# Attention and a mixture of experts on one core: the weighed V of a block issued one block later, behind the scores

## The reference

```python
x = x + _layernorm(attn(_layernorm(x), Wq, Wk, Wv, Wo))
x = x + _layernorm(ffn(_layernorm(x), router_w, Wg, Wu, Wd, ...))

def attn(x, Wq, Wk, Wv, Wo):
    q, k, v = proj(Wq), proj(Wk), proj(Wv)        # (B, H, S, 32)
    q, k = rope(q), rope(k)
    scores = where(causal, q @ k.T / sqrt(32), -big)
    probs = softmax(scores)
    return (probs @ v) @ Wo.T
```

## Time and profile before

| | before |
|---|---|
| median of 3 runs | 1199.74 us (1198.04 to 1199.86) |
| the profiled execution's own time | 1199.09 us |
| its span | 1197.2 us |
| mean granted TensorE clock | 0.968 |
| PE busy | 1085.3 us (91%) |
| DVE busy | 692.3 us (58%) |
| POOL busy | 621.0 us (52%) |
| ACT busy | 473.2 us (40%) |
| first `turn` and last `weighted` of the attention | 36.92 and 430.4 us |

### The profile page before, as it was taken

One profiled execution on the slowest core, in us unless ns is written; L12 is line 12 of the kernel. 1 busy time (PEld: TensorE's weight loads), 2 busy tenths in 40 slices (PEclk: granted clock), 3 DMA queues, 4 the chain that ended last, 5 costly groups with the idle time before them and its releaser, 6 DMA issues.

```text
span 1197.2 us, 24385 instructions
## 1 busy us (share of the span) xinstructions
PE 1085.3 (91%) x6309; PEld 728.9 (61%) x6310; DVE 692.3 (58%) x2354; ACT 473.2 (40%) x1366; POOL 621.0 (52%) x629
## 2 busy tenths in 40 slices
PE   5799899989999989979869999999999999999964
PEld 3455566555566545555537777777777776767721
DVE  3766566556666668857855454444444444444447
ACT  1566567656666642242202222222222222222213
POOL 4333333333333312200127888888888777778824
PEclk9899999999999999979969999999999999999987
DMA  9600000000000051100157999999999989997796
GB/s 350 241 2 1 4 1 2 2 4 2 1 2 1 2 227 55 62 16 12 60 163 173 223 218 248 244 226 235 258 231 255 242 213 269 259 227 160 113 318 251
DMA packets 65713, 166.81 MB, mean 139 GB/s; under 512 B 15314, under 2 KB 16594, under 8 KB 65504
## 3 DMA queue, kind: packets, MB, share of 16 engines
q0 software_dynamic: 38496, 83.95, 31.8%
q1 hardware_dynamic: 27136, 81.88, 19.4%
HBM read 119.85 MB, written 62.65 MB: 152 GB/s over the span
## 4 chain that ended last, share of the span: by engine, by line
PE 68%; DMA 16%; DVE 9%; issue 3%; ACT 2%; POOL 1%; DVEq 0%; POOLq 0%; ACTq 0%
PE ps L906 14%; PE ps L658 14%; DMA sum_rows<-x_t,idx 9%; PE ps L917 7%; PE ps L717 6%; DMA x_t<-x_rows,idx 5%; PE ps L773 4%; PE ps L687 4%; PE ps L890 4%; PE ps L737 4%; PE ps L672 2%; PE ps L809 2%; PE ps L789 1%; PE ps L825 1%; DVE high L1196 1%
## 5 line engine op out<-in xcount | busy, mean ns | idle before, releaser
L906 PE MATMUL ps<-big,work 128*128 x1264 | 300.5, 381 | 0.0
L430 POOL DMA_INDIRECT sum_rows<-x_t,idx x157 | 249.9, 1591 | 56.4 <-issue 37.4
L906 PEld LDWEIGHTS ps<-big,work 128*128 128x128 f32 x1264 | 229.0, 191 | 24.9
L424 POOL DMA_INDIRECT x_t<-x_rows,idx x159 | 165.9, 1043 | 69.9 <-issue 28.3
L658 PE MATMUL ps<-big 128*128 128x384 f32 x512 | 179.1, 493 | 1.5 <-ACT big L501 1.1
L369 POOL TENSOR_TENSOR work<-qkv_all,rope_sb 128x256 f32<-128x256 f32 x64 | 46.6, 728 | 249.4 <-ACT qkv_all L506 249.3
L612 ACT ACTIVATE work<-ps 128x512 f32<-128x512 f32 x159 | 94.9, 597 | 202.7 <-PE ps L890 200.4
L917 PE MATMUL ps<-big,work 128*128 x314 | 160.7, 593 | 0.3 <-issue 0.3
L890 PEld LDWEIGHTS ps<-ident_sb,x_t 128*128 128x128 f32 x636 | 78.1, 142 | 108.6 <-issue 68.3
L998 DVE CUSTOM_DVE_ANT_0 ps<-ps,mask_sb 128x128 f32<-128x128 f32 (+3 forms) x256 | 120.8, 513 | 24.0 <-PE ps L687 23.4
L523 ACT ACTIVATE work<-ps,neg_max 128x128 f32<-128x128 f32 (+3 forms) x256 | 132.4, 528 | 4.3 <-DVE neg_max L998 3.2
(11 more groups left out here) (176 smaller groups left out, 1455.9 us busy)
## 6 DMA issues: line engine op xcount, KB each, us to landing
big<-experts SPq DMA_DIRECT2D x65, 768.0 KB, 7.3
sum_rows<-x_t POOLq DMA_DIRECT2D x4, 2048.0 KB, 10.6
big<-sum_rows SPq DMA_DIRECT2D x8, 768.0 KB, 10.9
x_sb<-x SPq DMA_DIRECT2D x4, 1024.0 KB, 15.5
x_rows<-work SPq DMA_DIRECT2D x16, 256.0 KB, 2.0
sum_rows<-attn_t POOLq DMA_DIRECT2D x2, 2048.0 KB
out<-x_sb SPq DMA_DIRECT2D x16, 256.0 KB, 5.9
x_t<-sum_rows SPq DMA_DIRECT2D x4, 768.0 KB, 13.5
```

Of the source, the lines that this page charges most:

```text
L424: pool.indirect_dma_start(rows[:, q, :], None, x2_rows, bass.IndirectOffsetOnAxis(ap=idx[:, q, 0:1], axis=0), bounds_check=last_row, oob_i ...
L430: pool.indirect_dma_start(all_sums, bass.IndirectOffsetOnAxis(ap=idx[:, q, 1:2], axis=0), y_sb[:, q, :], None, bounds_check=last_sum, oob_ ...
L906: mm = pe.matmul(ps[:, 2 + p, 0:GATEUP], rows_t[:, p, c, :], w_ring[:, slot, c * GATEUP:(c + 1) * GATEUP], start=(c == 0), stop=(c == DC - 1))
```

## The change

`weigh` of block k-1 is issued in iteration k directly behind `score` of block k+1, in place of `weigh` of block k at the iteration's end; the last block of a batch is weighed at the end of its batch. `weigh` has a new wait, for `s_qkt` up to the copy of block k+2, since it now writes bank 6 behind `qkt`. `qkt` waits no longer for `weighted` of block k-1, but for `evac_rden` of block k-1 and `weighted` of block k-2. `turn_rden` keeps its wait for `weighted` of block k-1. On DVE `weighted` of block k-1 stands between the first and the second `masked` of block k+1. No operation is added or dropped.

```diff
--- before.py
+++ after.py
@@ -659,14 +659,18 @@
                                    start=(c == 0), stop=(c == DC - 1))
                 mm.then_inc(s_qkv_ps, 1)
 
-            def qkt(n, t, k):
+            def qkt(n, t, k, late=False, after=None):
 
                 pe.wait_ge(s_rope, n + 1)
+                if late:
+                    pe.wait_ge(s_rden_t, k)
+                    if after is not None:
+                        pe.wait_ge(s_attn, after)
                 if isinstance(n, int) and n < LEAD_QKT:
                     pe.wait_ge(s_qkv, TB - 1)
                 if not (isinstance(n, int) and n == 0):
                     pe.wait_ge(s_qkt, n)
-                if k is not None and not (isinstance(k, int) and k == 0):
+                if k is not None and not late and not (isinstance(k, int) and k == 0):
                     pe.wait_ge(s_attn, k)
                 for c in range(2):
                     mm = pe.transpose(turn_bank[:, bass.ts(c, P)], roped[:, t % 2, bass.ts(c, P)], ident_sb[:, :])
@@ -725,12 +729,13 @@
                     pe.wait_ge(s_attn, k)
                 pe.transpose(rden_bank, rden[:, :, :].rearrange("p h d -> p (h d)"), ident_sb[:, :]).then_inc(s_rden_ps, 1)
 
-            def weigh(k, i):
+            def weigh(k, i, qkts):
 
                 g, qt = divmod(i, TB)
                 pe.wait_ge(s_pt, (k + 1) * ON_ACT)
                 pe.wait_ge(s_pt_dve, k + 1)
                 pe.wait_ge(s_rden_t, k + 1)
+                pe.wait_ge(s_qkt, qkts)
                 for c in range(qt + 1):
                     for h in range(HG):
                         v0 = 2 * P + DH * h
@@ -743,21 +748,25 @@
 
                 for i in range(BLOCKS):
                     k = b * BLOCKS + i
+                    qkts = b * BLOCKS + min(i + LEAD_QKT + 1, BLOCKS) if last else b * BLOCKS + (i + LEAD_QKT + 1)
                     turn(k, i, 0)
                     turn(k, i, 1)
                     if i + LEAD_QKT < BLOCKS or not last:
-                        qkt(b * BLOCKS + (i + LEAD_QKT), (i + LEAD_QKT) % TB, k)
+                        qkt(b * BLOCKS + (i + LEAD_QKT), (i + LEAD_QKT) % TB, k, late=(i >= 1),
+                            after=b * BLOCKS + (i - 1) if i >= 2 else None)
                     if i + 1 < BLOCKS or not last:
                         score(b * BLOCKS + (i + 1), (i + 1) % BLOCKS)
+                    if i >= 1:
+                        weigh(b * BLOCKS + (i - 1), i - 1, qkts)
                     if i >= BLOCKS - TB and not last:
                         xt((b + 1) * TB, i % TB, qkv_bank)
                     turn(k, i, 2)
                     turn(k, i, 3)
-                    turn_rden(k, b * BLOCKS + min(i + LEAD_QKT + 1, BLOCKS) if last else b * BLOCKS + (i + LEAD_QKT + 1))
+                    turn_rden(k, qkts)
                     if i < BLOCKS - TB or not last:
                         proj(b * BLOCKS + (i + LEAD_PROJ), (i // TB + 1) % G, i % TB, qkv_bank,
                              after_xt=(b + 1) * TB if i >= BLOCKS - TB else None)
-                    weigh(k, i)
+                weigh(b * BLOCKS + (BLOCKS - 1), BLOCKS - 1, qkts)
 
             every_batch(pe, batch)
 
@@ -1033,12 +1042,16 @@
                         take_qkt(b * BLOCKS + j, j // TB % G, j % TB)
                     if more:
                         masked(k1, q1, 0)
+                    if i >= 1:
+                        weighted(b, b * BLOCKS + (i - 1), i - 1)
+                    if more:
                         masked(k1, q1, 1)
                     evac_pt(k, i)
                     if more:
                         masked(k1, q1, 2)
                         masked(k1, q1, 3)
-                    weighted(b, k, i)
+                    if i == BLOCKS - 1:
+                        weighted(b, k, i)
                     if more:
                         invert(k1)
                     if i in NORM_X_AT and not last:
```

## The result

Slower by a third of a percent: 1202.97 us against 1198.04 (medians of 7 runs each), ratio 1.0034 with a 95% interval of 1.0021 to 1.0048. That is 4.1 us by the ratio and 4.9 by the medians. A second set (12 runs against 28) gives 1.0035 (1.0019 to 1.0052); one more run of the kernel before, at 1984.34 us with a granted clock of 0.70, is left out there.

A forecast was written before the change was run, and what follows sets the result against it. The prediction took PE as the chain, packed to about 97% in the attention. Looped batches +1.0, last batch +0.9 and tail +0.9 gave +2.8 us: 1202.5 against 1199.74 us, +0.23%, range 1196.5 to 1207.5.

The forecast's parts named there:

- the slower case: Whole kernel a little slower, as summed: 0.5 to 5 us, chance 0.50; slower in all 0.48.
- The prize: PE's stalls before `qkt`, 0.42 us in q0 and 0.20 in q1, go: some 0.62 us in 23.6 of a group.
- The order of shapes: On PE `proj` is followed by `turn` instead of `weigh`, 2.58 us instead of 2.67: -0.1 a block.
- nothing saved: Rival: the order of shapes on PE saves nothing, +0.1 in 45 blocks, +4.5 us, 1207; chance 0.13.
- the rule of the Trainium skill: Weight loads overlap matmuls in flight only in different row groups, so `turn` behind `proj` on PE would save nothing.
- The stall in front of `weigh`: On PE `weigh` waits for DVE's copy of Q and K behind `invert`: 0.38 us in q3, 0.45 more behind `norm_x`.
- The stall in front of `turn_rden`: On PE `turn_rden` waits for `weighted` of block k-1: 0.42 us in q0, 0.35 in q1, 0.05 in q2, none in q3.
- Late starts: In block 8 of looped batches `weighted` starts 0.34 us later, half taken as lost (-0.17); rival "no difference", chance 0.22.
- The sum: Attention terms together: looped batches +0.33 each, +1.0 for three, last batch +0.9, tail +0.9: +2.8 us.
- tail: Last three blocks, without projection: `weigh` lies behind `score`, in front of the next link of the exps' chain: +0.9 us.
- the first rival: Faster: the copy of Q and K is not late, no stall in front of `weigh`: -5.7 and -2.7 us, 1194; chance 0.15.

The follow-up runs named there:

- e7: Changed kernel with the hardware loop over the first three batches written out; 1190.45 us, ratio 0.9945 to the kernel before.
- e9: e4 with Q and K of block k+2 turned between head 0 and head 1 in q3 blocks; ratio 0.9927 to the kernel before.
- e2: e1 with the reciprocals of every q3 block made behind the copy of Q and K; ratio 0.9988 to the kernel before.
- e1: Changed kernel with `norm_x` issued ahead of `invert` instead of behind it; ratio 1.0019 to the kernel before.
- e4: e2 plus the tail of e3 and, in q1 blocks, the multiplication of the block before ahead of the first mask; ratio 0.9937 to the kernel before.
- e8: Kernel before with the hardware loop over the first three batches written out; 1183.51 us, ratio 0.9893 to the kernel before.
- e6: Kernel before with every reciprocal made twice; ratio 1.0162 to the kernel before.
- e0: Changed kernel run again as it is, as base of the first group; ratio 1.0035 to the kernel before.
- e3: Changed kernel with blocks 12 to 15 of the last batch weighed at the end of their own iteration, as before; ratio 1.0010 to the kernel before.
- e5: Changed kernel with every reciprocal made twice; ratio 1.0250 to the kernel before.
- the corrected one: The kernel of e9, changed order with all corrections; with the loop written out 1175.03 us, ratio 0.9823 to the kernel before.

## Why the prediction held, and where it did not

Direction and size held: +0.23% was forecast and +0.34% measured, and the slower case had the largest chance. That 1202.5 and 1202.97 us lie so near each other is luck: the base came out at 1198.04 instead of 1199.74, and the difference was 4.1 to 4.9 us instead of 2.8.

- *The prize.* `qkt` follows `turn` after 0.22 in q0 and 0.44 in q1 (forecast 0.27 and 0.49).
- *The order of shapes.* `proj` to `turn` is 2.58 us behind a q3's projection and in the whole last batch, as forecast from the one row ahead of the loop; behind the projections of the looped q0 to q2 it is 2.65, which saves 0.02 instead of 0.09. Why is open. A stalled `turn_rden` in front is not the reason, since it stalls in the last batch as well; without the loop (e7) it is 2.58 everywhere. The term holds all the same, by a saving that was not forecast: from `proj` to `score`, less `weigh`, a looped q2 takes 3.62 where it took 3.71, since `qkt` and `score` follow a little sooner as well (0.65 and 0.31, before 0.71 and 0.32). `score` to `weigh` costs what `score` to `turn` did (0.43 to 0.44 in e9). So the rival "nothing saved" is out, and with it the rule of the Trainium skill that I set against this term ("TensorE: Matmul & The Clock Gate", Part 3), as I had read it: here weights for all rows were loaded under a running projection (the load of q3's first `turn` starts at 182.16 and its matmul at 182.48, and the projection runs from 179.83 for 2.81). The same Part of the Trainium skill also lets the load of a background weight buffer go ahead of matmuls in flight; I had left that out, and the trace fits it.
- *The stall in front of `weigh`.* Forecast 0.38 in q3, found 0.34 to 0.44; with `norm_x` 0.8 to 0.9 (forecast 0.83). The size is right, the cause half: I worked out 4.63 by way of exps and `invert`, and left out that `qkt` and the copy alone need 0.99 against 0.74. e2 showed it, e9 removed it. I also missed block 14, whose copy stands behind the `norm_x` of block 13: 0.2 each (e1).
- *The stall in front of `turn_rden`.* Forecast 0.42 in q0, the old one at another place, and 0.35 in q1. Found: 0.68 and 0.85 from `turn` to `turn_rden`, where the forecast comes to 0.69 and 0.85. e4 took 0.15 to 0.26 of q1 away by putting the multiplication ahead of the mask.
- *Late starts.* I took half of block 8's 0.34 as lost. All of it was won, 6.10 to 5.61. e8 shows that these starts come with the loop: without it the old order has 5.63 there. Why they occur stays open.
- *The sum.* Looped batches from block 2 on +1.2 (forecast, with block 1, +1.0), last batch +0.5 (+0.9), tail +0.9 (+0.9). Together 2.6 for a forecast of 2.8, but the terms miss in both directions and cancel: the looped blocks lost some 0.4 more (block 14 above all, against block 8), the last batch 0.4 less. What I had no term for is the first block of a round, +1.15, and the pauses, +0.2.

One premise of the stall in front of `weigh` was misread and came true by luck. The prediction takes the four exps to follow each other every 0.68 us and to end at 3.2, and says against the first rival that they do so without a gap. In the kernel before, the third waited 0.47 for its mask:

```profile
180.95 0.69 ACT L523 ACTIVATE work<-ps,neg_max 128x512 f32<-128x512 f32 x1 [0.47 <-DVE neg_max L998]
```

There the four ended 3.69 behind the projection of 178.62 (the last ran from 181.63 to 182.31). In the changed kernel `weigh` stands between the scores and `turn`, so that DVE is through with its masks earlier against the projection, and the exps end at 3.21 (182.36 + 0.68, projection at 179.83).

The first block of a round is seen and not explained, and it is not shown to belong to the change. Block 1 of the second and third round lasted 6.12 and 5.79 us in the kernel before, and 5.96 and 6.86 in e6, which has the old order too. With the new order the pairs are 5.73 and 7.18 (5.80 and 7.29 in e0, 5.78 and 7.09 in e3), but also 6.00 and 5.81 (e5), 6.38 and 6.98 (e1), 7.00 and 7.03 (e2), 7.08 and 7.02 (e4), 7.21 and 6.15 (e9). In the trace shown above it is time at the low clock, and it goes with the loop. It does not make the loss: e7 and e8 have neither pause nor long block there and lie 7 us apart. The waits and places of the forecast carry 2.6 us; what the measured 4.1 to 4.9 us have beyond them stays open; the first block of a round may be a part of it.

## What to carry to other kernels

When an operation is moved to fill a gap, list what it will wait for at its new place, and add up the shortest path to that (here transposes, a copy and two semaphores, 0.99 us) against the time in which the engine gets there (0.74): a wait that used to end behind long work may become the first one. Tiles that share a PSUM bank under semaphores, as here, pass such waits on to each other, and what stands on the other engine ahead of the releasing instruction (here `invert` and `norm_x`) is suddenly on the path; put ahead of it only what it needs, and let the rest fill the time in which that engine waits.
A bracket in a profile can name the wrong releaser: look up the semaphores in the code, and let an experiment say it.

## What was not expected of the hardware

The loop itself costs more than the whole change: written out it gave 12.5 us in the old order (1196.04 to 1183.51) and 13 in the corrected one (1188.25 to 1175.03). The traces of the old order (before and e8) are 13.6 us apart in the attention: 8.3 of them lie in the two blocks 0 with PE's pauses between rounds, 1.1 in the blocks 1 behind them, and 4.2 in blocks 2 to 15, which the loop makes longer as well (q0 5.75 against 5.63).

And in four of the profiled executions the granted clock fell in the tail, in which PE pauses for 0.8 to 1.0 us at a time. From the projection of block 11 to the last `weigh` it was 0.93 in e1 (22.9 us long), 0.86 in e7 (23.9), and 0.93 and 0.85 in e5 and e6 (23.9 and 23.1, in part for the doubled reciprocals); e6 has the old order of work. In all the other profiles it was 1.00 there, also in the two of the changed kernel, whose last batch does the same work in the same order as e1's and took 21.4. What decides it stays open.
